# Where the divisions stand in short experts, bias rows added by matmul, and unread matmuls ahead of the output product

## The reference, cut to what matters

```python
h   = _ln(xf, ln1_w, ln1_b)                   # per expert
q, k, v = split(h @ ipw.T + ipb)              # 8 heads of 64 columns
a   = softmax(where(mask, q @ k.T / 8, NEG))
o   = (a @ v) @ opw.T + opb                   # opb: first bias row, 512 values
x1  = xf + o
h2  = _ln(x1, ln2_w, ln2_b)
m   = gelu(h2 @ w1.T + b1) @ w2.T + b2        # b2: second bias row, 512 values
return x1 + m
```

## Time and profile before

| | |
|---|---|
| median of 3 runs | 1335.82 us (1334.84 to 1337.59) |
| the profiled execution, its own time | 1336.74 us |
| its span, first to last instruction | 1334.7 us |
| mean granted TensorE clock | 0.884 of full speed |
| busy: PE, DVE, ACT, POOL | 1025.8, 749.8, 453.7, 375.2 us |
| experts | from about 421 us to the end |

### The profile page before, as it was taken

One profiled execution on the slowest core, in us unless ns is written; L12 is line 12 of the kernel. 1 busy time (PEld: TensorE's weight loads), 2 busy tenths in 40 slices (PEclk: granted clock), 3 DMA queues, 4 the chain that ended last, 5 costly groups with the idle time before them and its releaser, 6 DMA issues.

```text
span 1334.7 us, 19087 instructions
## 1 busy us (share of the span) xinstructions
PE 1025.8 (77%) x4940; PEld 571.0 (43%) x4941; DVE 749.8 (56%) x1557; ACT 453.7 (34%) x843; POOL 375.2 (28%) x340
## 2 busy tenths in 40 slices
PE   1987699998801876677776888979799779978874
PEld 1654477777800333333334433434344335533323
DVE  5395425441462368745685465674856537835654
ACT  1301121221312355234625423434434452235522
POOL 2102324441366163414342033000000125413212
PEclk9987799998555988889977888989999989989978
DMA  4291000000427114221333010000000312110010
GB/s 147 62 292 43 1 2 0 0 0 1 156 66 236 70 48 146 66 85 32 111 108 123 6 61 4 1 0 0 0 0 7 113 48 64 66 63 1 9 31 33
DMA packets 33792, 76.71 MB, mean 57 GB/s; under 512 B 6373, under 2 KB 6671, under 8 KB 33433
## 3 DMA queue, kind: packets, MB, share of 16 engines
q1 hardware_dynamic: 25405, 58.05, 14.0%
q0 software_dynamic: 8000, 15.44, 4.0%
q10 hardware_dynamic: 288, 2.10, 0.4%
HBM read 52.72 MB, written 24.13 MB: 58 GB/s over the span
## 4 chain that ended last, share of the span: by engine, by line
PE 62%; DVE 16%; issue 11%; ACT 5%; POOL 3%; DMA 1%; DVEq 1%; SPq 0%; ACTq 0%; POOLq 0%
PE bank L1346 14%; PE bank L1437 8%; PE bank L1221 8%; PE bank L1260 5%; PE bank L1467 4%; PE bank L1522 3%; PE bank L1256 2%; PE bank L1401 2%; PE bank L1422 2%; PE bank L1424 2%; PE bank L1187 2%; DVE den L2157 2%; POOL lists L658 1%; PE bank L1481 1%; PE bank L1506 1%
## 5 line engine op out<-in xcount | busy, mean ns | idle before, releaser
L1795 DVE TENSOR_SCALAR oh_src<-iota,edge 125x1250 f16 x178 | 101.8, 572 | 107.1 <-PE bank L1221 102.3
L1437 PE MATMUL bank<-probs_t,v_head 128*128 128x512 f32 (+1 forms) x288 | 148.5, 600 | 7.0 <-ACT probs_t L1006 6.4
L1006 ACT ACTIVATE probs_t<-bank 128x512 f32<-128x512 f32 x144 | 81.5, 573 | 141.6 <-PE bank L1424 141.1
L562 POOL TENSOR_TENSOR w<-w_stage,w 128x1024 f16<-128x1024 f32 x40 | 86.7, 2182 | 146.4 <-ACT w L819 146.4
L2080 DVE TENSOR_REDUCE mx<-bank 128x1 f32<-128x512 f32 x144 | 88.1, 656 | 69.6 <-PE bank L1401 69.0
L1221 PE MATMUL bank<-oh_src,oh_dst 125*125 x534 | 112.0, 361 | 2.7 <-DVE oh_dst L1797 0.7
L1522 PE MATMUL bank<-probs_t,v_head 128*128 128x128 f32 (+2 forms) x192 | 90.2, 555 | 7.7 <-ACT probs_t L1057 6.0
L1346 PE MATMUL bank<-hT,w 128*128 128x256 f16 (+1 forms) x552 | 89.5, 326 | 1.6 <-DVE hT L2013 1.6
L1221 PEld LDWEIGHTS bank<-oh_src,oh_dst 125*125 x534 | 71.1, 143 | 43.7 <-issue 24.6
L1346 PE MATMUL bank<-w,oT 128*128 128x512 f16 x264 | 67.3, 421 | 26.4 <-DVE oT L2160 17.3
L1467 PE MATMUL bank<-hT,w 128*128 128x512 f16 x288 | 76.6, 401 | 7.8 <-ACT t L1031 7.8
(11 more groups left out here) (300 smaller groups left out, 1978.3 us busy)
## 6 DMA issues: line engine op xcount, KB each, us to landing
w_stage<-in_ew_dram SPq DMA_DIRECT2D x40, 512.0 KB, 3.8
lists<-zeros SPq DMA_DIRECT2D x1, 10340.0 KB, 50.0
x_in<-lists SPq DMA_DIRECT2D x20, 517.0 KB, 6.5
x_mem<-lists SPq DMA_DIRECT2D x3, 1024.0 KB, 8.3
x_mem<-lists SPq DMA_DIRECT2D x1, 2560.0 KB, 11.5
out_dram<-x_mem SPq DMA_DIRECT2D x10, 250.0 KB
big<-in_x_dram SPq DMA_DIRECT2D x10, 224.0 KB
x_mem<-in_x_dram SPq DMA_DIRECT2D x1, 2240.0 KB
```

The costliest lines, as they stand in the source:

```text
L562: nc.gpsimd.tensor_tensor(w16[:, 1, cols], w_stage[:, p % WB, :], w16[:, 0, cols], ALU.subtract).then_inc(s_elo, 1)
L1006: nc.scalar.activation(probs_t[:, x % NPB, 0:cn], stb[x % 2][:, 0:cn], ACT.Exp).then_inc(s_exp, 1)
L1437: nc.tensor.matmul(pvb[(hd * nq + s) % 2][:, 0:cn], v_head[:, hd, kt, :], probs_t[:, (hd * nx + i) % NPB, 0:cn], start=(k == 0), stop=(k = ...
L1795: nc.vector.tensor_scalar(oh_src[:, bass.ds(slot, 1), i, 0:N].rearrange("p a n -> p (a n)"), iota[:, :], edge[:, 0, i, bass.ds(g, 1)], Non ...
```

## The change

It has four parts.

1. In `short_pair`, all parts of the division of pair j-1 stand directly after the maxima of head 2j+1 (before the key split), none at the end of the pair.
2. Both bias rows are added on PE. `bias_rows` holds each in two 16-bit halves on partitions 0 and 32 with zeros between, `ones_k` holds ones, and `product` begins its accumulation with one matmul of 33 rows by 512 columns. `add_bias`, the additions at L789 and the waits for them are gone from POOL, SP and DVE; SP loads two rows into `den`, after a wait for the end of the expert before (`s_given`), and DVE makes the halves in `bias_halves`, four small operations. ACT (ahead of its first exponential) and PE (ahead of the output product) wait for them by `s_bias`. Two memsets are added in the routing stage.
3. Between an expert's last value sum and its output product PE issues 18 (short) or 32 (long) matmuls of 512 columns that nothing reads.
4. DVE's `residual` waits for the loaded rows instead of the added bias, and `part` no longer waits for POOL.

```diff
@@ sp
                 sp.dma_start(x1[:, 0:nt, :], list_rows).then_inc(s_xr, 16)
+                sp.wait_ge(s_given, e + 1)
+                for b in range(2):
+                    sp.dma_start(den[LOW * b:LOW * b + 1, 0:D], erow[bass.ds(e, 1), b, :]).then_inc(s_rp, 16)
                 with sp.If(e < NE - 1):
                     for p in range(WB):
                         load_piece(e + 1, p)
...
-                sp.dma_start(row_par[:, :], erow[bass.ds(e, 1), 1, :].partition_broadcast(P)).then_inc(s_rp, 16)
@@ pool
             nc.gpsimd.memset(total_rows[:, :, :], 0.0).then_inc(s_econst, 1)
+            nc.gpsimd.memset(bias_rows[:, :], 0.0).then_inc(s_econst, 1)
+            nc.gpsimd.memset(ones_k[:, :], 1.0).then_inc(s_econst, 1)
...
                     second_head(1)
-                    add_bias()
...
-                    add_bias()
                     summed.settle()
...
-                    pool.wait_ge(s_n2, normed.at(2 * p + 2))
-                    for t in (2 * p, 2 * p + 1):
-                        nc.gpsimd.tensor_tensor(x1[:, t, :], x1[:, t, :], row_par[:, :], ALU.add).then_inc(s_b2, 1)
@@ act, short expert
                     row_of(0)
-                    act.wait_ge(s_given, e + 1)
+                    act.wait_ge(s_bias, e + 1)
                     for u in range(H):
                         short_head(u)
@@ pe
+            def product(bank, lhs, rhs, chunks, bias=None):
+                if bias is not None:
+                    nc.tensor.matmul(bank, ones_k[0:LOW + 1, :], bias, start=True, stop=False)
...
+                for k in range(WARM_SHORT if shape.short else WARM_LONG):
+                    nc.tensor.matmul(sbk[k % 2][:, :], ident_h[:, :], hT[0][:, k % KC, 0:512], start=True, stop=True)
...
+                pe.wait_ge(s_bias, e + 1)
@@ dve
+                def bias_halves():
+
+                    dve.wait_ge(s_rp, e * 32 + 32)
+                    for b in range(2):
+                        raw, cols = den[LOW * b:LOW * b + 1, 0:D], slice(b * D, (b + 1) * D)
+                        step(nc.vector.tensor_copy(bias_rows[0:1, cols], raw))
+                        last = nc.vector.tensor_tensor(bias_rows[LOW:LOW + 1, cols], raw, bias_rows[0:1, cols],
+                                                       ALU.subtract)
+                    last.then_inc(s_bias, 1)
...
                     maxima_of(2 * j + 1)
-                    if j > 0 and nq > 1:
-                        divide_of(j - 1, 0)
+                    if j > 0:
+                        for s in range(nq):
+                            divide_of(j - 1, s)
                     if j < 3:
                         split_of(j + 1, 1)
                         second_of(j + 1)
...
                         owners(e, nt)
-                    if j > 0:
-                        divide_of(j - 1, nq - 1)
...
                     maxima_of(0)
                     second_of(0)
+                    bias_halves()
...
                     second_head_copies()
+                    bias_halves()
...
-                        dve.wait_ge(s_xb, biased.at(nt))
+                        dve.wait_ge(s_xr, e * 16 + 16)
...
-                    dve.wait_ge(s_b2, b2_done.at(t + 1))
```

More of the change, by code:

```diff
@@ L55 @@
 SHORT = 512
+LOW = 32
+WARM_SHORT, WARM_LONG = 18, 32
 UP = 5
@@ L288, in program @@
         t32 = sb("t32", [P, 2, 512], F32)
-        row_par = sb("row_par", [P, D], F32)
+        bias_rows = sb("bias_rows", [P, 2 * D], F16)
+        ones_k = sb("ones_k", [P, P], F16)
         ep_ln1 = sb("ep_ln1", [P, 2 * KC], F32)
@@ L422, in program @@
         s_m2 = sem("s_m2")
-        s_b2 = sem("s_b2")
+        s_bias = sem("s_bias")
         s_part = sem("s_part")
@@ L508, in _ @@
             sp.wait_ge(s_arms, 1)
-            sp.wait_ge(s_econst, 10)
+            sp.wait_ge(s_econst, 12)
             def load_rows(e):
@@ L691, in after_head @@
                     pool.sem_inc(s_idle, 1)
[L693 to L697, removed]
                 def values_of(j, hd):
@@ L807, in expert_pool @@
                 pool.sem_inc(s_given, 1)
-                for r in (copied, stats, normed, summed, added, gathered, splits, returned_up, seconds):
+                for r in (copied, stats, summed, added, gathered, splits, returned_up, seconds):
                     r.settle()
@@ L905, in _ @@
             act.wait_ge(s_routed, 1)
-            act.wait_ge(s_econst, 10)
+            act.wait_ge(s_econst, 12)
             act.sem_inc(s_taken, 2)
@@ L1314, in _ @@
             pe.wait_ge(s_routed, 1)
-            pe.wait_ge(s_econst, 10)
+            pe.wait_ge(s_econst, 12)
             pe.wait_ge(s_slots, 1)
@@ L1341, in _ @@
             PASSES = [(0, 0), (1, 0), (0, 1)]
-            def product(bank, lhs, rhs, chunks):
+            def product(bank, lhs, rhs, chunks, bias=None):
+                if bias is not None:
+                    nc.tensor.matmul(bank, ones_k[0:LOW + 1, :], bias, start=True, stop=False)
                 for n, (a, b) in enumerate(PASSES):
                     for c in range(chunks):
-                        last = nc.tensor.matmul(bank, lhs(a, c), rhs(b, c), start=(n == 0 and c == 0),
+                        last = nc.tensor.matmul(bank, lhs(a, c), rhs(b, c), start=(n == 0 and c == 0 and bias is None),
                                                 stop=(n == 2 and c == chunks - 1))
@@ L1631, in project_out @@
                     product(sbk[t % 2][:, :], lambda a, c: oT[a][:, c, t * P:(t + 1) * P],
-                            lambda b, c: w16[:, b, W_OUT + c * D:W_OUT + (c + 1) * D], KC).then_inc(s_attn, 1)
+                            lambda b, c: w16[:, b, W_OUT + c * D:W_OUT + (c + 1) * D], KC,
+                            bias_rows[0:LOW + 1, 0:D]).then_inc(s_attn, 1)
                 def turn_second(p):
@@ L1969, in _ @@
             dve.wait_ge(s_epar, 17)
-            dve.wait_ge(s_econst, 10)
+            dve.wait_ge(s_econst, 12)
             dve.sem_inc(s_split, 2)
@@ L1984, in _ @@
             on = Tally(dve, "dve_on", 2)
-            biased = Tally(dve, "dve_biased", 0)
             heads = Tally(dve, "dve_heads", 1)
@@ L1995, in _ @@
             mixed = Tally(dve, "dve_m2", 0)
-            b2_done = Tally(dve, "dve_b2", 0)
             parts = Tally(dve, "dve_parts", 0)
-            counts = [heads, taken, seconds, steps, scored, maxed, scored_t, on, biased, affine, attn, x1_done, normed,
-                      turned, gelued, mixed, b2_done, parts, sides]
+            counts = [heads, taken, seconds, steps, scored, maxed, scored_t, on, affine, attn, x1_done, normed,
+                      turned, gelued, mixed, parts, sides]
             def step(ins):
@@ L2318, in expert_dve @@
                         give(2 * k - 5)
-                for r in (biased, affine, attn, x1_done, turned, mixed, b2_done, parts, results):
+                for r in (affine, attn, x1_done, turned, mixed, parts, results):
                     r.skip(nt)
```

14 lines of the change are left out of this document (2 added, 12 removed).

## The result

The changed kernel takes 1325.48 us (median of 4 runs, 1324.23 to 1326.71) against 1335.33 us of the kernel before beside it: a ratio of 0.992, 95% interval 0.990 to 0.994. Faster by 10 us, inside the range of 1303 to 1333; the predicted time was 5.5 us too low. The profiled execution took 1324.23 us, its span is 1322.5 us, its granted clock 0.897.

The account below looks back on a forecast made before the run. PE was taken as the bound, losing time idle for DVE or at the lower clock. Gains of 21.0 (heads) and 2.3 (unread matmuls) less 7.7 (bias matmuls) made 15.6 us, so 1320 us, range 1303 to 1333.

Parts of the forecast that it names:

- Waits in the heads: PE's waits for DVE in short experts' heads: idling and clock falls drop from 46.4 to 25.4 us, gaining 21.0.
- the nine places: PE's waits in heads 2, 4 and 6 of three short experts: 31.1 us idle before, 16.9 after.
- the additions' leaving: Without POOL's bias additions, the first wait of each short expert falls to 2.0, 2.0 and 1.0 us.
- this meeting: POOL's weight subtraction falls near pair 1's moved division in short experts, adding 1.0 us, 0.8 in the last.
- Bias rows on PE: Added bias matmuls in the output stages, 0.216 us each, lose 7.7 us, bounds 6 and 9.5.
- The signs to look for: Profile signs expected after the change, among them long-expert output steps of 12.2 us in place of 11.32.
- Making the halves: DVE's four small operations cost 0; in the long expert bounds are 3 us gained and 4 lost.
- The unread matmuls: Filling PE's gaps before output products gains 2.3 us: 1.15 last expert, 0.6 long, 0.3 each first two.
- The second rival: Unread matmuls before the output products do nothing: 2.3 us less gain, 1322.5 us; chance 0.59 together with the likeliest case.
- SP's wait, memsets: SP's wait for the previous expert's end and two memsets in the routing stage: each taken as 0.

Follow-up runs that it names:

- Run 1: Kernel before with only the divisions moved to their new place: 1317.37 us, ratio 0.985 to the kernel before.
- run 2: Changed kernel with the divisions at their old places and no unread matmuls, so only the bias rows by matmul: 1341.11 us, ratio 1.003 to the kernel before.
- run 3: Changed kernel without the unread matmuls, so moved divisions and bias rows by matmul: 1330.94 us, ratio 0.996 to the kernel before.
- Run 8: Changed kernel with POOL's low weight halves in short experts' heads made for only 16 columns of each piece (output not the reference's): 1313.69 us, ratio 0.982.
- run 7: Changed kernel with early halves and bias matmuls of 64 rows in place of 33: 1316.22 us, mean of 2 runs (1311.87 and 1320.57).
- run 6: Run 4 with bias matmuls of 128 rows, 96 of them zero, in place of 33: 1307.26 us, ratio 0.977 to the kernel before.
- run 4: Changed kernel with the long expert's bias halves made ahead of its first maxima, not behind the second-head copies: 1316.12 us, ratio 0.986 to the kernel before.
- run 5: Kernel before with moved divisions and the 18 or 32 unread matmuls, bias rows still added on POOL: 1316.95 us, ratio 0.985.
- run 11: Run 6 with more unread matmuls, 30 in the short expert with one query part and 40 in the long one: 1308.08 us, ratio 0.978.
- run 12: Run 11 with the division in three places, reciprocals before the key split, the rest before and behind the maxima of head 2j+2: 1298.99 us, ratio 0.973.

## Why the prediction was right, and where its terms were off

**Waits in the heads: the sum right, by luck in part.** Where 16.9 us of idling should stay in the nine places, 15.6 us are there by the timeline (7.4 in the first short expert, 5.7 in the second, 2.5 in the last), and the waits are those that were named: the key split in pairs 1 and 2, some 1.5 us in head 2 (0.5 in the last). So idling fell by 15.5 us (14.2 forecast), and the low clock by 17.2 us (44.4 to 27.2), of which half, 8.6, had been lost (6.8 forecast): the last expert kept 1.00 all through its heads. The heads give 24.6 us against 21.0.

But this total was reached by two errors that cancel. By the prediction's terms the divisions are worth 9.8 us of the 21.0 (6.4 of idling, two falls of the clock) and the additions' leaving 11.2. Run 1 shows 18.8 us for the divisions alone, run 2 15.7 us for the bias part alone, 34.5 together, and the changed kernel has 24.6: each term was too small, and the forecast added what is partly one gain (run 3). The lateness of pair 1 is not fixed by the division; it depends on where the heads have shifted against POOL's weight subtraction, and on the clock that PE comes with. The prediction had this meeting as a fixed 1.0 us. Run 8 prices the subtractions at 11 us.

**Bias rows on PE: the step that failed.** "so each further one 0.216 us at 2.4 GHz; the 0.39 us is one with 66 rows, so 33 rows save nothing" took the price of 33 rows from a row with 66. With 66 rows the next matmul does start 0.22 us later (lines under run 7). With 33 rows it costs 0.43 us, twice the term, and runs 6 and 7 show that it is the height. Of the 7.7 us forecast the output stages show 10.2 us of loss, and that with the low clock there shortened by the unread matmuls; in run 3 against run 1, without them, the part cost 13.6 us net of what it saved in the heads (16.4 us longer output stages). The signs to look for said steps of 12.2 us; they were 12.97, and are 12.12 with 128 rows (1105.62 to 1117.74).

**Making the halves: off within its bounds.** Taken as 0 with 3 gained to 4 lost. In the changed kernel the stretch ahead of the long expert's heads loses 2.9 us, and the heads 0.9. The 2.9 us are mostly not the halves' price: with the halves made early (run 4) 2.3 of them stay. The real price lies in the heads: taking the additions off POOL had opened a gain of 10 us there, which ACT's wait for the halves closed again (run 4). The prediction saw both (6 us earlier, and "ACT ... now waits for the halves") and set them against each other; it didn't see that they were separable by one line.

**The unread matmuls: right in sign, 2.3 us forecast, 5.5 measured.** The second rival (they do nothing) fell for this kernel but holds with the bias rows on POOL (run 5). The forecast had 0.3 us each in the first two experts, because the second product waits for the division; with the bias rows on POOL the first of them shows that. With bias matmuls of 33 rows in front, 1.4 and 1.5 us came there (14.35 to 12.95 and 14.44 to 12.94 us from the output product to the first transposes, run 3 against the changed kernel), and another 1.5 in the last. In the last expert 3.04 us of idling still brought 4.00 us for the first product, as forecast (run 6 shows that it needn't be so).

**SP's wait, memsets: taken as 0.** The balance doesn't bear this out or refute it: 1.5, 2.9 and 0.6 us, 5.0 in all, are lost ahead of the heads of the second, third and last expert. Of these, 3.1 us are DVE's longer idle time ahead of an expert's first operation: 14.4 and 14.2 us over three changes of expert in the kernel before and run 1, 17.5 to 18.0 in the changed kernel and runs 2 to 4. It was not forecast, and its cause stays open; no run takes SP's wait out by itself.

**Sum.** 15.6 us forecast, 12.2 by the spans: 3.6 more in the heads of short experts; 3.8 less for the long expert's start and heads; output stages 10.2 longer, where bias and unread matmuls together were forecast at 5.4, so 4.8 less; 2.8 more by heads of the first expert that begin earlier, which is within the spread; about 1 less in the rest. That 12.2 stands so near 15.6 is luck too: single terms were off by 3.6 to 4.8 us, in both directions.

## What to carry to other kernels

Before adding small matmuls to a dense stream on PE, look at their height: one of 33 or 64 rows between matmuls of 128 rows cost 0.43 us, one of 66 rows or padded with zeros to 128 rows 0.22. A price is only as good as the row it is read from: the one of 66 rows did not stand for one of 33. Where an order on DVE is changed, cut the moved work to the gap that is there (a gap of 3.3 us took 3.5 us of reciprocals, and the waits for the key split in the heads went), and put the rest into the next gaps. When a wait is put in front of an engine, ask for the earliest place where its data could be made; here moving four small operations was worth nearly as much as the whole change (9.4 and 9.9 us).

## What the runs showed of the hardware that was not expected

- A matmul of 33 or 64 rows costs 0.1 us at the change from 128 rows and 0.1 us at the change back, one of 66 rows nothing at either; its own row in the trace (0.39 us) hardly shows it, only the starts do.
- Clock gained at one place can be lost at the next: with no low clock in the first products of the long expert, 3.4 us of it came later in the same stage (run 11; 3.5 in run 12), and run 5 removed 23.8 us of low clock for no time that could be measured.
- The same idling of 3.04 us ahead of the last expert's output product was followed by 3.4 us at the low clock in the changed kernel and by none in run 6.
- Two changes that each remove a wait can share one gain: 7.7, 8.3 and 7.5 us of waiting in the same three heads with the divisions moved, with the bias rows moved, and with both.
